# Second attention: one phase for relative terms and scores, by half units of two heads, with stores by 64 rows

## The reference

```python
q, k, v = heads(x @ Wq + bq), heads(x @ Wk + bk), heads(x @ Wv + bv)     # 16 heads, D = 8
scores = einsum('bhqd,bhkd->bhqk', q, k)
pos_emb = dist_emb[pos_l - pos_r + M - 1]                                # (512, 512, 8)
rel_q = einsum('bhld,lrd->bhlr', q, pos_emb)
rel_k = einsum('bhrd,lrd->bhlr', k, pos_emb)
probs = softmax((scores + rel_q + rel_k) / sqrt(D))
out = layernorm(merge(probs @ v) @ Wo + bo + x)
```

## Time and profile before

| | us |
|---|---|
| median of three runs | 4914.96 (4913.7 to 4920.73) |
| profiled execution, its own time | 4912.15 |
| its span in the trace | 4910.4 |
| PE, DVE, ACT, POOL busy in it | 3915.1, 2889.9, 2635.3, 1689.6 |

### The profile page before, as it was taken

The page is one execution under the profiler, slowest core; times in us unless marked ns, Lnnn a source line. Parts: engine busy times, 40 slices in busy tenths (PEclk is TensorE's granted clock), DMA queues, the critical chain, the costliest instruction groups (busy, mean ns, idle before and its releaser), DMA issues.

```text
span 4910.4 us, 102424 instructions
## 1 busy us (share of the span) xinstructions
PE 3915.1 (80%) x31924; PEld 2380.9 (48%) x31924; DVE 2889.9 (59%) x6305; ACT 2635.3 (54%) x6550; POOL 1689.6 (34%) x1383
## 2 busy tenths in 40 slices
PE   2999999999488888734666565999999945888886
PEld 1555555554255555522222222677777723555554
DVE  2555555555577777543444443566666665777775
ACT  1555555554367777523333333566666624777774
POOL 0000000000588888523222222111111116878774
PEclk9999999999799999965555555999999977999998
DMA  3222222221111111027999999777777711111111
GB/s 118 87 78 78 78 78 80 81 78 53 49 25 23 27 27 23 17 71 293 380 381 385 380 381 369 269 262 260 248 272 250 256 43 52 25 26 25 25 23 32
DMA packets 374686, 701.06 MB, mean 143 GB/s; under 512 B 54180, under 2 KB 161016, under 8 KB 374568
## 3 DMA queue, kind: packets, MB, share of 16 engines
q1 hardware_dynamic: 330536, 565.25, 33.6%
q0 software_dynamic: 44032, 134.30, 7.4%
HBM read 336.53 MB, written 314.64 MB: 133 GB/s over the span
## 4 chain that ended last, share of the span: by engine, by line
PE 51%; DMA 13%; DVE 10%; issue 9%; POOL 7%; ACT 4%; SPq 2%; DVEq 1%; POOLq 0%; ACTq 0%
DMA rel_k<-b_stage_k 12%; PE ps L332 5%; PE ps L1465 5%; PE ps L340 5%; PE ps L351 5%; PE ps L1474 5%; PE ps L1456 3%; PE ps L1485 3%; DVE f_rs L1028 2%; POOL f_rn L758 2%; PE ps L866 2%; DVE f_rc L1025 2%; POOL f_rot L756 2%; PE ps L1357 2%; DVE b_stage_k L1381 2%
## 5 line engine op out<-in xcount | busy, mean ns | idle before, releaser
L1381 DVE COPY b_stage_k<-ps 128x640 f32<-128x640 f32 (+2 forms) x512 | 359.1, 722 | 469.6 <-DMA rel_k<-b_stage_k 410.3
L430 ACT ACTIVATE a_p<-a_s,a_min 128x512 f32<-128x512 f32 x512 | 366.0, 715 | 470.3 <-DVE a_min L474 470.3
L1378 ACT ACTIVATE b_stage_q<-ps 128x640 f32<-128x640 f32 (+2 forms) x512 | 316.0, 624 | 505.4 <-PE ps L1360 388.0
L474 DVE CUSTOM_DVE_ANT_0 a_s<-ps,a_table 128x512 f32<-128x512 f32 x512 | 333.5, 689 | 374.5 <-PE ps L332 371.9
L1539 ACT ACTIVATE c_p<-c_s,c_min 128x512 f32<-128x512 f32 x512 | 370.2, 723 | 290.7 <-PE ps L1474 180.3
L1357 PE MATMUL ps<-b_e,b_st_k 48*128 48x512 bf16 (+1 forms) x512 | 305.9, 597 | 261.1 <-DVE b_stage_k L1381 261.1
L1574 DVE CUSTOM_DVE_ANT_0 c_s<-ps,c_rq 128x512 f32<-128x512 f32 x512 | 352.8, 689 | 200.8 <-PE ps L1465 188.1
L188 POOL COPY y<-ln_rows 128x512 f32 x32 | 19.9, 621 | 1304.8 <-DVE ln_rows L180 1304.8
L949 ACT ACTIVATE f_p<-f_s,f_min 128x128 f32<-128x128 f32 x1024 | 396.3, 390 | 89.1 <-DVE f_min L1014 88.7
L756 POOL TENSOR_TENSOR f_rot<-f_rc,f_rs 128x1024 f32<-128x1024 f32 x128 | 302.9, 2367 | 255.6 <-DVE f_rs L1028 255.3
L758 POOL TENSOR_TENSOR f_rn<-f_ss,f_power 128x16 f32<-128x16 f32 x128 | 373.8, 2920 | 14.9 <-DVE f_ss L1037 1.4
(11 more groups left out here) (171 smaller groups left out, 9194.5 us busy)
## 6 DMA issues: line engine op xcount, KB each, us to landing
rel_q<-b_stage_q SPq DMA_DIRECT2D x64, 1280.0 KB, 7.8
rel_k<-b_stage_k SPq DMA_DIRECT2D x64, 1280.0 KB, 7.7
c_rq<-rel_q SPq DMA_DIRECT2D x64, 1024.0 KB, 7.7
c_rk<-rel_k POOLq DMA_DIRECT2D x64, 1024.0 KB, 11.9
a_table<-skew_bias SPq DMA_DIRECT2D x64, 896.0 KB, 4.6
f_vb<-f_v SPq DMA_DIRECT2D x256, 128.0 KB, 2.4
rel_k<-b_stage_k SPq DMA_DIRECT2D x32, 1024.0 KB, 9.5
rel_q<-b_stage_q SPq DMA_DIRECT2D x32, 1024.0 KB, 5.3
```

Of the source, the lines that this page charges most:

```text
L430: nc.scalar.activation(a_p[:, lt % 2, h, :], a_s[:, lt % 2, h, :], ACT.Exp, bias=a_min[:, lt % 2, h:h + 1], scale=-1.0, accum_out=a_sum[:, ...
L1381: moves_b1(dve, 1, lambda out, src: nc.vector.tensor_copy(out, src))
```

## The change

b1 and b2 become one phase, and the barrier between them goes. The unit keeps four heads but is worked in two **halves** of two heads (`HALF`); tile `a` is now half `a // 8`, row tile `(a % 8) // 2`, head `a % 2`.

- In step `a` of unit `s` PE also makes the relative terms of tile `a` of unit `s + 1`: their first piece (up to 512 columns) ahead of the transposes, the second (128 columns, which q has in row tiles 0 and 1, k in 2 and 3) after the scores. Each of q and k has one PSUM bank for it (`REL_BANKS`), so a piece waits until the piece before it has been moved. ACT and DVE move piece by piece (`move_rel`): 24 moves a unit each in place of 16.
- The scores go into two banks in place of four, and run two tiles ahead in place of three.
- `stack_qk` is gone. The stack stays in `b_st`, which has four slots of half a unit, loaded by 24 transfers a unit in place of 12.
- A stage slot holds two heads. Its store is two transfers of 64 rows, each without the 64 columns that no skewed read touches: widths of 576, 576, 448 and 320 columns for q in place of 640, 640, 512 and 384, and the same for k in the other order. That is 32 transfers a unit in place of 8.
- `c_rk` has two slots of half a unit. It is loaded for a half when all k stores of the half have landed. `c_rq` has one slot, and its loads are by two heads.
- Unit 0's relative terms stand ahead of the loop; the last unit has none beside it. The values of a row tile are multiplied after steps 11, 13 and 15 and after step 1 of the next unit.

The core of the diff:

```diff
-    def sync_b1_loads(pool):
...
-                sp.dma_start(stack_dram[u, n], b_st[n][:, q, :, :]).then_inc(b_st_stored[q], 16)
...
+    SCORE_BANKS, PT_BANK, MIX_BANK, REL_BANKS, JOIN_BANK = [0, 1], 2, 4, [5, 6], 7
...
+        def load_rk(u, hf):
+            for r in range(2):
+                hold(pool, b_rel_stored[1][r], u * 128 + (hf * 64 + 96))
+            for rt in range(LT):
...
+                pool.dma_start(c_rk[:, hf, rt, :, 0:hi - lo], src).then_inc(c_rk_loaded[hf], 16)
+
+        def step(s, q, first, last):
+            hold(pool, c_scored, s * TILES + 32)
+            load_rk(s, 1)
+            if not last:
+                load_stack(s + 1, 1 - q, 1)
...
+            if not last:
+                hold(pool, c_scored, s * TILES + (32 + PART))
+                load_rk(s + 1, 0)
+                load_stack((s + 2) % UNITS_B, q, 0)
...
+        def store_rel(u, hf, lt):
+            for n in range(2):
+                lo, hi = near(n, lt)
+                hold(sp, b_rel_moved[n], u * PIECES + (piece_no(n, hf * PART + lt * HALF + HALF) + 1))
+                for g in range(2):
+                    f, w = (1 - g) * (P // 2), hi - lo + P // 2
...
+                    sp.dma_start(dst, b_stage[n][g * (P // 2):(g + 1) * (P // 2), lt % 2, :, f:f + w]
+                                 ).then_inc(b_rel_stored[n][lt % 2], 16)
...
+        def step(s, q, first, last):
+            for hf in range(2):
+                for lt in range(LT):
+                    if hf == 0 or not last:
+                        hold(sp, c_biased, s * TILES + (hf * PART + lt * HALF + HALF + 24))
+                        load_rq(s + hf, 1 - hf, lt)
+                    if not last:
+                        store_rel(s + 1, hf, lt)
...
+            for n in range(2):
+                for f, t in pieces(n, lt)[part:part + 1]:
+                    x = at + near(n, lt)[0]
+                    pe.wait_ge(b_rel_moved[n], u * PIECES + (piece_no(n, a) + part + 1))
+                    nc.tensor.matmul(ps[:, REL_BANKS[n], 0:t - f], b_st[n][:, 2 * q + hf, h, lt * P:(lt + 1) * P],
+                                     b_e[:, n, x + f:x + t], start=True, stop=True).then_inc(b_rel_full[n], 1)
...
+            for a in range(TILES):
+                if not last:
+                    relative(s + 1, 1 - q, a, 0)
+                transpose_probs(s, a)
+                if a + AHEAD < TILES:
+                    scores(s, q, a + AHEAD)
+                elif not last:
+                    scores(s + 1, 1 - q, a + AHEAD - TILES)
+                if not last:
+                    relative(s + 1, 1 - q, a, 1)
...
+        for f, t in pieces(n, lt)[part:part + 1]:
+            eng.wait_ge(b_rel_full[n], u * PIECES + (piece_no(n, a) + part + 1))
+            move(b_stage[n][:, lt % 2, h, f:t], ps[:, REL_BANKS[n], 0:t - f]).then_inc(b_rel_moved[n], 1)
...
             for a in range(TILES):
+                if not last:
+                    move_rel(dve, 1, s + 1, a, 0, move)
                 if a + 2 < TILES:
                     bias_and_min(s, q, a + 2)
...
                     nc.vector.tensor_copy(out, src).then_inc(c_pT_slot[0].emptied, 1)
+                if not last:
+                    move_rel(dve, 1, s + 1, a, 1, move)
```

More of the change, by code:

```diff
@@ new lines, in tensor_b1, with relative @@
+    def tensor_b1(pe):
+        AHEAD = 2
+        def relative(u, q, a, part):
+            hf, lt, h = place(a)
+            at = EW - WIN - lt * P
+            if lt == 0 and h == 0 and part == 0:
+                pe.wait_ge(b_st_loaded[2 * q + hf], (u // 2) * 192 + 192)
+            for n in range(2):
+                for f, t in pieces(n, lt)[part:part + 1]:
[3 more added lines that the diff above has]
+                                     b_e[:, n, x + f:x + t], start=True, stop=True).then_inc(b_rel_full[n], 1)
+        def scores(u, q, a):
+            hf, lt, h = place(a)
+            r, sl = SCORE_BANKS[a % 2], 2 * q + hf
+            far = near(0, lt)[0]
+            if lt == 0 and h == 0:
+                pe.wait_ge(c_rk_loaded[hf], u * 64 + 64)
+            pe.wait_ge(c_biased, u * TILES + (a + 23))
+            queries = b_st[0][:, sl, h, lt * P:(lt + 1) * P]
+            nc.tensor.matmul(ps[:, r, :], queries, b_st[1][:, sl, h, :], start=True, stop=False)
+            if far > 0:
+                nc.tensor.matmul(ps[:, r, 0:far], queries, b_e[:, 0, 0:1].broadcast_to([STACK, far]), start=False, stop=False)
+                nc.tensor.matmul(ps[:, r, 0:far], b_e[:, 1, EW - 2:EW - 1].broadcast_to([STACK, P]), b_st[1][:, sl, h, 0:far],
+                                 start=False, stop=False)
+            for rt in range(far // P, LT):
+                last = nc.tensor.matmul(ps[:, r, rt * P:(rt + 1) * P], c_rk[:, hf, rt, h, lt * P:(lt + 1) * P],
@@ L1603, in step @@
                     nc.vector.tensor_copy(out, src).then_inc(c_pT_slot[0].emptied, 1)
+                if not last:
+                    move_rel(dve, 1, s + 1, a, 1, move)
                 if a == 0 and not first:
                     invert_sums(s - 1, 1 - q)
-                if a == 5 and not first:
+                if a == 6 and not first:
                     move_out(s - 1, 1 - q)
@@ L1609, in step @@
                     add_to_y(s - 1)
+        dve.wait_ge(c_pad, LT - 1)
+        for a in range(TILES):
+            for part in range(2):
+                move_rel(dve, 1, 0, a, part, move)
         bias_and_min(0, 0, 0)
```

289 lines of the change are left out of this document (118 added, 171 removed).

## The result

The changed kernel takes **5497.32 us** (median of four runs, 5490.95 to 5537.84), the kernel before 4914.33 beside it: a ratio of 1.1201, 95% interval 1.1146 to 1.1257. It is slower by 583 us where 104 us less were forecast, and the time lies far outside the range. The profiled execution took 5490.95 us with a span of 5489.1.

The account below looks back on a forecast made before the run. The prediction took DMA to bound b1 and PE b2, 53 us a unit; merged, a 48.0 us chain of waits plus 2 of store waits gave 50, 31 units and ends 1649 for 1752: 4810 us, range 4670 to 4935.

Parts of the forecast that it names:

- The sum: Whole kernel: 31 joint units at 50 us plus ends, 1649 us for 1752, so 103 us less.
- PE loses its clock: Rival for the joint phase: 79 us a unit at half clock, 4990 with a fifth of units so; chance 0.03.
- The chain: Waits between PE, ACT and DVE over the joint unit's 16 steps, at full clock: 48.0 us a unit.
- The stores: Term stores as two of 64 rows without unread columns: 20.3 us a unit for 23, nothing taken for splitting.
- the 48 us a unit that I worked out from its fixed cost for each transfer: Splitting cost by the skill's rule: 24 more transfers a unit at 2.0 us each, if one after another.
- The stage waits: Store waits in the joint unit beyond what the chain hides: 2 us a unit, bounds 0 and 3 a half.
- The late read of `rel_k`: Rival: first scores of a half wait for `c_rk`, 4.7 us each, unit 57.4, time 5039; chance 0.12.
- The short chain: Rival: engines overlap better, DMA sets the pace, joint unit 42 us, time 4562; chance 0.05.
- the balance at 53 a unit: Rival "It nets out": store waits 1 to 2 us more a half, 53 a unit, no difference; chance 0.04.
- my list of signs: Joint phase: period 48 to 51 us, DMA share 0.80 to 0.85, PEclk 1.00; patchy PEclk would show it wrong.

Follow-up runs that it names:

- e1: Changed kernel plus four bf16 products of 48 rows x 512 columns at the head of each step, results overwritten: 5905.63 us, ratio 1.2047.
- e5: Changed kernel plus four bf16 products of 128 rows x 512 columns at the head of each step, results overwritten: 5345.24 us, ratio 1.0879.
- e6: Changed kernel plus twelve fp32 128x128 transposes at the head of each step, results overwritten: 5374.52 us, ratio 1.0939.
- e13: Changed kernel with both stacks and the table of distances padded with zeros from 48 to 128 rows: 5035.92 us, ratio 1.0242.
- e16: Changed kernel with stacks and table padded to 128 rows, whole stores of 128 rows and four stage slots in place of two: 4749.06 us, ratio 0.9658.
- e17: Changed kernel with whole stores and four stage slots, stacks and table left at 48 rows: 5364.98 us, ratio 1.0915.
- e15: Kernel before, with stack and table of the scores phase padded with zeros from 48 to 128 rows: 4798.89 us, ratio 0.9762.
- e3: Kernel before, each store of relative terms as two transfers of 64 neighbouring rows, without the 64 unread columns: 5100.60 us, ratio 1.0381.
- e7: Kernel before, each store cut into two transfers of 64 neighbouring rows with all columns: 5172.69 us, ratio 1.0528.
- e4: Changed kernel with the store splitting undone, one store of 128 rows with all columns for a stage slot: 5435.47 us, ratio 1.1067.
- e14: Changed kernel with stacks and table padded to 128 rows and whole stores of 128 rows: 4963.64 us, ratio 1.0092.
- e11: Kernel before, each store cut into two transfers of every second row, all columns: 4918.51 us, ratio 1.0005.

## Why the prediction was wrong

- **The step that failed: the clock.** The sum has PEclk at 1.00 and takes nothing for its loss; it was 0.63, and 19 of the 21.9 us missed in a unit are that. I had the rival "PE loses its clock" at 0.03, on "a cold PE is busy almost throughout" and on b2 at 0.99. e1 refutes the first: busy 0.97, clock 0.62. b2 was the wrong row to carry over. It has products over 48 rows too, but one to three for each group of transposes, where the new phase has four to six in a step; that its transposes and products over 128 rows hold its clock is what e5 and e6 suggest, and no run of b2 shows it. The row that spoke stood in the text: b1 has only products over 48 rows and 0.50 at a busy share of 0.60, while other work kept 0.89 at 0.61. I read both as busy shares and left the difference unexplained. e1 and e5, e13, and e16 beside e17 settle that the rows count: padding moves the clock from 0.62 to 0.84 with two slots, and from 0.65 to 0.92 with four. PE's waits behind k's small piece have their part, since the clock falls there with either height.
- **The rival's price was right.** 79 us a unit at half clock was forecast, 79.8 measured. I gave it a fifth of the units, and three quarters of the phase's time ran so, a part of every unit.
- **The chain was nearly right.** 48.0 forecast, 50.5 at full clock. The 2.5 are 0.15 us in each of 16 steps: transposes and scores together 1.49 for 1.34, probably from more changes between 48 and 128 rows (e15 shows their price).
- **The stores were mis-sized.** I took nothing for splitting and 20.3 us by bytes. In the kernel before, where stores set b1, trimming with halves costs 191 us (e3), halves alone 256 (e7), each against the kernel before beside it. In the changed kernel they cost 62 (e4) and, padded, 72 (e14). The Trainium skill's rule against two halves (DMA: Bandwidth & Descriptors, Rules for kernel authors) has the direction of e7 right; the 48 us a unit that I worked out from its fixed cost for each transfer was no measure: 32 units of e7, with 8 transfers more a unit, lose 8 us each, and e11, with as many more, loses nothing.
- **The stage waits** were about what I took, 2 us a unit, while the clock was down (2.4 left over above). They were mis-sized for the case that I forecast: with the clock mostly up, four slots save 215 us, 7 a unit. Such a stall also starts the fall of the clock in the timeline above; e17 shows that without stalls it falls all the same.
- **The late read of `rel_k`** (0.12) did not occur: no wait of PE is put down to it. Each read lands in 6.8 us for the 11.9 assumed, and steps at half clock leave more time. Its price was also built on 48 us a unit and not on my 50.
- **The short chain** and the balance at 53 a unit were not reached. e16, at 47.3, shows that one phase can pay, with rows of 128, whole stores and four slots; that is not the kernel that was forecast. From e15 to e16, 4798.89 to 4749.06, is what the merge itself is worth over a kernel of two phases with padded scores: 50 us.
- Of my list of signs, the patchy PEclk was the one that told it, and the DMA share of 0.70 in place of 0.80 to 0.85 goes with it (0.83 in e13).

**Open:** what heights between 48 and 128 rows do, since no run has one in this phase. Whether it is the unused rows of the array, or something that goes with them in such a product, that keeps the clock down; zeros in these rows raise it. By what the gap at a change between 48 and 128 rows comes about. Whether a store of one half is slow for its partitions or for its rows in DRAM. And what the stalls of some 4 to 5 us are in loops with fillers.

## What to carry to other kernels

The clock that PE is granted has to be forecast from what kind of matmul fills the stretch, not only from how busy PE is: if products use 48 of 128 rows, pad the operands with zeros in a copy that is made once, before anything else is tried. Expect more from it where steps leave PE waiting: there the clock falls, and with 128 rows it came back sooner. Where a stretch runs at half clock in the trace of before, ask why before moving its work into a stretch at full clock, because it may take that clock along. Split a store by columns or by alternating rows, not into the lower and upper 64 partitions, and give a stage that is stored while it is filled more slots once the engines are fast.

## What the runs showed of the hardware that was not expected

- Four products over 48 rows more a step: PEclk 0.62 to 0.62, with PE busy 97%; over 128 rows: 0.93. Rows of zeros: 0.84, with no product added.
- Twelve transposes more a step: 0.97, though they are said not to count.
- The clock falls in the same step of nearly every unit (step 4, 30 of 48 falls), stays at 0.50 through steps 5 to 8 with products over 48 rows, and with rows of zeros is back at 0.95 by step 8.
- A change between products over 48 rows and transposes over 128 costs some 0.1 us: 1.34 to 1.09 us a tile at full clock.
- A packet of 2560 bytes in a store of 64 neighbouring partitions takes 142.3 ns for 104.2; of every second partition, 103.9.
